# A graph attention layer's first two stages rearranged: layer norm after the projection, node starts counted on TensorE, the score table read in quarters

## What is computed

```
def _L0_gnn_ref(x, edge_index, W, att_src, att_dst, bias, gamma, beta):   # x is already layer-normed
    xh = (x @ W).reshape(N, H, D)                       # H = 8 heads, D = 32
    a_src = jnp.einsum('nhd,hd->nh', xh, att_src)
    a_dst = jnp.einsum('nhd,hd->nh', xh, att_dst)
    ... src, dst = the edges, and a loop on each node
    e = jax.nn.leaky_relu(a_src[src] + a_dst[dst], 0.2)
    m = jax.ops.segment_max(e, dst, N);  e = jnp.exp(e - m[dst])
    alpha = e / segment_sum(e, dst, N)[dst]
    out = segment_sum(xh[src] * alpha, dst, N) + bias
    ... batch norm over the nodes, + x
```

## Time and profile before

| | |
|---|---|
| median of 3 runs | 1977.33 us (1975.37 to 1977.82) |
| profiled execution | 1977.53 us, of which the span from first to last instruction is 1975.8 us |
| first stage | VectorE's next block begins at 100.73 us |
| second stage | the block after it begins at 163.43 us |
| busy over the span | TensorE 69%, GpSimd 56%, VectorE 46%, ScalarE 29% |
| granted TensorE clock, mean | 0.823 of 2.4 GHz |

### The profile page before, as it was taken

How to read it: one execution, slowest core, us unless ns; L and a number is a source line. 1 busy time by engine, 2 the same in 40 slices (tenths; PEclk the granted TensorE clock), 3 DMA queues, 4 the chain that set the end, 5 groups by cost and what they waited for, 6 DMA issues and landing times. The chain is left out here.

```text
span 1975.8 us, 23808 instructions
## 1 busy us (share of the span) xinstructions
PE 1365.6 (69%) x6688; PEld 1134.1 (57%) x6688; DVE 907.3 (46%) x1818; ACT 576.3 (29%) x1264; POOL 1098.3 (56%) x1086
## 2 busy tenths in 40 slices
PE   2435666656666266599999997656666666567998
PEld 2324544444454146599999997444445444346787
DVE  7425544444443667633333333644334333335953
ACT  2133433323333014133333332422222222222310
POOL 4477777777774600377222273077777777773520
PEclk7756878878878575699999999877878787978999
DMA  6484998888887601432111122743333333330002
GB/s 145 119 251 150 298 312 284 281 285 272 276 283 258 155 6 63 134 115 83 46 46 46 46 98 65 174 142 104 105 105 105 105 104 105 106 99 1 1 1 65
DMA packets 156809, 268.56 MB, mean 136 GB/s; under 512 B 26747, under 2 KB 119839, under 8 KB 155567
## 3 DMA queue, kind: packets, MB, share of 16 engines
q1 hardware_dynamic: 100252, 135.75, 22.1%
q0 software_dynamic: 46224, 123.97, 21.0%
q10 hardware_dynamic: 10213, 7.36, 1.5%
HBM read 169.82 MB, written 98.15 MB: 136 GB/s over the span
## 5 line engine op out<-in xcount | busy, mean ns | idle before, releaser
L1182 POOL DMA_INDIRECT sum_rows<-xn_tab,src_e x391 | 373.3, 955 | 174.5 <-issue 118.8
L1207 PE MATMUL bank<-sum_held,sum_hot 128*125 128x256 f32 x976 | 304.1, 474 | 195.3 <-ACT sum_held L1217 191.1
L798 POOL DMA_INDIRECT gat_rows<-xh_tab,src_e x363 | 343.4, 946 | 114.8 <-issue 107.8
L1207 PEld LDWEIGHTS bank<-sum_held,sum_hot 128*125 128x125 f32 x976 | 222.2, 236 | 273.5 <-issue 179.7
L871 PE MATMUL bank<-gat_rows,gat_same 128*128 128x264 f32 x784 | 263.7, 483 | 126.2 <-issue 126.2
L871 PEld LDWEIGHTS bank<-gat_rows,gat_same 128*128 128x128 f32 x784 | 176.6, 244 | 166.4 <-issue 132.6
L1217 ACT COPY sum_held<-sum_rows 128x1024 f32 x122 | 127.4, 1045 | 373.6 <-SPq L1173 334.1
L1894 PE MATMUL bank<-weights,e_xthigh 128*128 x896 | 220.3, 330 | 8.5 <-DVE e_xtlow L2049 5.4
L915 ACT COPY gat_outs<-bank 128x528 f32<-128x528 f32 x196 | 117.3, 598 | 281.8 <-PE bank L871 280.5
L2054 DVE TENSOR_TENSOR e_h<-e_gated,bank 128x342 f32<-128x342 f32 x112 | 57.1, 510 | 262.9 <-ACT e_gated L1987 262.9
L1239 DVE SCALAR_TENSOR_TENSOR res<-bank,prep_inv,res 125x256 f32 x122 | 58.9, 483 | 234.8 <-PE bank L1207 228.2
(11 more groups left out here) (508 smaller groups left out, 2416.8 us busy)
## 6 DMA issues: line engine op xcount, KB each, us to landing
parts<-gat_outs SPq DMA_DIRECT2D x27, 1904.0 KB, 8.0
staged<-w_tab SPq DMA_DIRECT2D x8, 2132.0 KB, 8.9
w_tab<-w_stage SPq DMA_DIRECT2D x16, 682.0 KB, 10.6
w_raw<-in_L_ffn_w_dram SPq DMA_DIRECT2D x16, 640.0 KB
gat_rows<-xh_tab,src_e POOLq DMA_INDIRECT x391, 4.7
sum_rows<-xn_tab,src_e POOLq DMA_INDIRECT x391, 2.8
w_tab<-w_stage SPq DMA_DIRECT2D x8, 768.0 KB, 10.6
weights<-y_tab SPq DMA_DIRECT2D x10, 600.0 KB
```

The source lines that it names most:

```text
L798: pool.indirect_dma_start(out=rows[b % R][:, t, :], out_offset=None, in_=k.xh_tab, in_offset=bass.IndirectOffsetOnAxis(ap=k.src_e[:, b * S ...
L1182: pool.indirect_dma_start(out=rows[:, at // IP % (RING * GPAIRS), at % IP, :], out_offset=None, in_=k.xn_tab, in_offset=bass.IndirectOffse ...
L1207: m = nc.tensor.matmul(k.ps[s][0:P, 0:C], hot[g % 2][:, s, c, :], held[:, s, c, :], start=(c == 0), stop=(c == IP - 1))
```

## The change

First stage:

- `x` is loaded in five chunks, straight behind the edges on SyncE's queue. `dst_pad`, `start_tab`, the 25 window gathers on GpSimd and the 25 passes over all tiles are gone.
- TensorE transposes the raw `x`, tile by tile, and multiplies with a `w` whose column means have been taken off (one matmul with `ones`, two VectorE instructions). VectorE multiplies by `rstd` and adds the bias in one instruction as it takes the result out of PSUM. Layer norm statistics are taken chunk by chunk.
- `starts` are counted otherwise. ScalarE makes `passed` [98, 4, 3125]: the sign of (node - first `dst` of the tile), four `Sign` instructions of 3125 elements, at the head of its list and ahead of all its copies. VectorE makes `rises` [98, 4, 129]: the differences to the tile before, and a column of ones. For each of 25 node tiles TensorE adds four matmuls `passed` x `rises` in PSUM, which gives each node its window of 128 edges and the tile's number. These 100 matmuls come behind the whole projection in TensorE's list. VectorE and ScalarE count in the windows (two of each four tiles each). `end` comes from two small matmuls.
- SyncE stores `xh_tab` chunk by chunk and then `adst_tab`. GpSimd gathers `firsts` (4) behind the 14 gathers of batch 0, still in this block.

Second stage: SyncE loads `sparse` in four quarters, each with its own semaphore; VectorE scans each as it comes (4 x 8 scans of 128), and the transposes and copies go by eighths. The store of `tails` moves from ScalarE's queue to SyncE's, behind the quarters. `joins` is made in `Walk.on_vector` (three VectorE instructions for rows 0 to 7).

```diff
@@ first_phase, tables @@
-        trash = sb("trash", [P, NT, ET])
-        windows = sb("window", [128, NT, EP])
+        neg_first, rises = sb("neg_first", [Q, J]), sb("rises", [Q, J, WIN])      # WIN = 129
+        passed = sb("passed", [Q, J, N])
+        trash = sb("trash", [P, 8, EP])
@@ sync @@
-            sp.wait_ge(edges_f, 1)
-            sp.dma_start(k.dst_pad..., dstq[:, :]).then_inc(pad_out, 16)
-            move(sp, k.res[:, :, :], x, x_in)
+            for c in range(CHUNKS):
+                move(sp, k.res[:, c * TB:(c + 1) * TB, :], x_rows[:, c * TB:(c + 1) * TB, :], x_in[c])
+            sp.dma_start(bias[:, 0:C], ...)
...
+            for c in range(CHUNKS):
+                sp.wait_ge(taken, (c + 1) * TB)
+                move(sp, xh_rows[:, tiles, :], k.xh[:, tiles, 0:XW], xh_done)
+            for c in range(CHUNKS):
+                move(sp, adst_rows[:, tiles, :], k.xh[:, tiles, XW:RW], adst_out)
@@ scalar @@
-            for t in range(DVE_COUNTS, NT):
-                nc.scalar.activation(trash[:, t, :], first_b[0:P, :], ACT.Sign, bias=half[:, t:t + 1], scale=-1.0, ...)
-            norm_roots(k, act, deviations, roots)
+            act.wait_ge(eps_made, 1)
+            nc.scalar.activation(root0[:, :], eps[:, :], ACT.Sqrt)
+            act.wait_ge(numbered, 1)
+            act.wait_ge(firsts_made, 1)
+            for j in range(J):
+                nc.scalar.activation(passed[:, j, :], node_row, ACT.Sign, bias=neg_first[:, j:j + 1]).then_inc(passed_made, 1)
+            for c in range(CHUNKS):
+                for t in range(c * TB, (c + 1) * TB):
+                    ... nc.scalar.copy(xt[:, t % XR], k.ps[t % XR][:, 0:2 * P])
+                    if t % TB == 2: ... activation(k.rstd chunk, spread chunk, ACT.Sqrt, ...).then_inc(roots, 1)
+            for t in range(NT):
+                if t % WG >= BY_DVE:                                              # WG = 4, BY_DVE = 2
+                    nc.scalar.activation(trash[:, t % 8, :], k.ps[t % 8][0:P, 0:EP], ACT.Sign, ..., accum_out=before[:, t:t + 1])
@@ gpsimd @@
-            for t in range(NT):
-                pool.indirect_dma_start(out=windows[:, t, :], in_=k.dst_pad...)
+            nc.gpsimd.iota(node_row, pattern=[[1, N]], ...).then_inc(numbered, 1)
...
             gather_batch(k, pool, 0)
+            pool.wait_ge(adst_out, 32 * CHUNKS)
+            for j in range(J):
+                pool.indirect_dma_start(out=k.firsts[:, j, :], in_=k.adst_tab, ...)
@@ tensor @@
-            for i in range(NT // TB):   # transposes of xn, then matmuls, five by five
+            for c in range(2):
+                nc.tensor.matmul(k.ps[XR - 1][:, 0:RW], k.ones[:, :], w[:, c, :], ...)
+            for t in range(NT + 1):     # two transposes of k.res tile t, then two matmuls of tile t - 1
+                ...
+            pe.wait_ge(passed_made, J)
+            pe.wait_ge(rises_made, 1)
+            for t in range(NT):
+                ... wait for tiles_kept of two groups back
+                for j in range(J):
+                    nc.tensor.matmul(k.ps[t % 8][0:P, 0:WIN], passed[:, j, t * P:(t + 1) * P], rises[:, j, :], ...)
+            nc.tensor.matmul(k.ps[0][0:P, 0:NT], k.ident[0:P, 1:P + 1], start[:, 0:NT], start=True, stop=False)
+            nc.tensor.matmul(k.ps[0][0:P, 0:NT], corner[:, :], start[:, 1:NT + 1], start=False, stop=True)
@@ vector @@
-            for t in range(DVE_COUNTS):
-                v.tensor_scalar(trash[:, t, :], first_b[0:P, :], k.node[:, t:t + 1], None, ALU.is_lt, ALU.add, ...)
+            spreads(0); w -= column means; the five table copies
+            for c in range(CHUNKS):
+                if c < CHUNKS - 1: spreads(c + 1)     # bn_stats x5 and four small ones
+                take(c)                               # xh = ps * rstd + bias, x5
+                if c == 2: ... rises
+            for g in range(GROUPS): ... count in two windows, keep four tile numbers from PSUM
@@ spread_phase, sync @@
-            sp.dma_start(sparse[:, :], edge_rows).then_inc(sparse_in, 16)
+            for j in range(J):
+                sp.dma_start(sparse[:, part], edge_rows[:, part]).then_inc(sparse_in[j], 16)
+            sp.wait_ge(tails_made, 2)
+            move(sp, chain_rows[:, :, C:RW], tails[:, :, :], k.chain_cleared)
@@ gpsimd @@
-            for j in range(J):
-                pool.indirect_dma_start(out=firsts[:, j, :], in_=k.adst_tab, ...)
@@ scalar @@
-            act.wait_ge(tails_made, 2)
-            move(act, chain_rows[:, :, C:RW], tails[:, :, :], k.chain_cleared)
@@ vector @@
-            for h in range(H):
-                v.tensor_tensor_scan(filled[:, h::H], k.cont_q[:, :], sparse[:, h::H], ...)
+            for j in range(J):
+                dve.wait_ge(sparse_in[j], 16)
+                ... copy firsts of quarter j
+                for h in range(H):
+                    v.tensor_tensor_scan(filled_j[:, h::H], k.cont_q[:, j * EP:(j + 1) * EP], of_j[:, h::H], ...)
@@ Walk.on_vector @@
+        me(dve, v.memset(k.joins[0:H, 0:1], 0.0))
+        me(dve, v.tensor_copy(k.joins[0:H, 1:ET], self.bank[0:H, 0:ET - 1]))
+        me(dve, v.tensor_tensor(k.joins[0:H, 1:ET], self.bank[0:H, 1:ET], k.joins[0:H, 1:ET], ALU.is_equal))
```

More of the change, by code:

```diff
@@ L302, in _ @@
+            act.wait_ge(halves_made, 1)
+            for t in range(NT):
+                if t % WG >= BY_DVE:
+                    act.wait_ge(windows, t + 1)
+                    nc.scalar.activation(trash[:, t % 8, :], k.ps[t % 8][0:P, 0:EP], ACT.Sign, bias=half[:, t:t + 1], scale=-1.0,
+                                         accum_out=before[:, t:t + 1]).then_inc(signed, 1)
         @block.gpsimd
@@ new lines, in _ @@
+            for c in range(2):
+                last_mm = nc.tensor.matmul(k.ps[XR - 1][:, 0:RW], k.ones[:, :], w[:, c, :], start=(c == 0), stop=(c == 1))
+            last_mm.then_inc(w_summed, 1)
+            for t in range(NT + 1):
+                if t < NT:
+                    if t == XR - 1:
+                        pe.wait_ge(w_ready, 1)
+                    if t % TB == 0:
+                        pe.wait_ge(x_in[t // TB], 32)
+                    if t >= XR:
+                        pe.wait_ge(xt_made, t - XR + 1)
@@ new lines, in take @@
+            def take(c):
+                rstd = k.rstd[:, c * TB:(c + 1) * TB]
+                dve.wait_ge(roots, c + 1)
+                me(dve, v.reciprocal(rstd, rstd))
+                for t in range(c * TB, (c + 1) * TB):
+                    dve.wait_ge(projected, t + 1)
+                    v.scalar_tensor_tensor(out=k.xh[:, t, :], in0=k.ps[XR + t % XP][0:P, 0:RW], scalar=k.rstd[:, t:t + 1], in1=bias[:, :], op0=ALU.mult, op1=ALU.add).then_inc(taken, 1)
+            spreads(0)
+            dve.wait_ge(w_summed, 1)
```

363 lines of the change are left out of this document (171 added, 192 removed).

## The result

The changed kernel takes 1949.15 us in the median of four runs (1947.08 to 1950.14), beside 1976.35 us of the kernel before (four runs, 1971.5 to 1977.82): a ratio of 0.9859, 95% interval 0.9843 to 0.9876. I had forecast 1959.5 us with a range from 1951.5 to 1968.5.

The account below looks back on a forecast made before the run. GpSimd was taken to set the edge stage's pace, so the ends of the two stages ahead of it counted. The span of 1975.8 us less 12.8 and 5.1, plus 1.7, gave 1959.6, stated as 1959.5 us; range 1951.5 to 1968.5.

Parts of the forecast that it names:

- the price of a window matmul: First stage, TensorE: 200 instructions at 0.16 us each, 32 us, bounds 26 and 34.
- TensorE's chain: First stage: projection to 52.2 us, window matmuls to 84.2, then small work; it ends the stage at 87.9 us.
- The drain: Ends of both stages: a block ends 4.8 us after GpSimd's last indirect DMA starts.
- The slow gathers: Second stage: four gathers under VectorE's scans took 1.93 instead of 0.95 us; the 3.9 us lost was left unchanged.
- Both gains: First stage 12.8 us gained, bounds 7.8 and 17.6; second stage 5.1 us, bounds 0 and 8.
- the first case of the two that I had left open: First stage, ScalarE's head: ready at 18.6 us, or 21.2 if `Sqrt` ahead of `Sign` needs another table load.
- the scores' chain: Second stage: quarter loads, scans, transposes and copies, done 54.8 us into the block, ahead of GpSimd's 57.6.
- Rival A: Second stage: the store of the tails on SyncE ends at 62.4 us, nothing gained there: 1964.7 us; chance 0.1.
- B: First stage: the 200 matmuls run at the lower clock level, 52 us: 1979.6 us, no change; chance 0.04.
- C: First stage: TensorE stays at the lower clock level through projection and windows: 2008 us, slower; chance 0.03.
- D: First stage: VectorE's or ScalarE's head much later than 24 us, 5 us more: 1965 us; chance 0.08.
- TensorE's projection: First stage: 25 tiles at 1.21 us, 30.2 us, plus 1 us for beginning at the lower clock level.

Follow-up runs that it names:

- e1: The kernel before with only the new first stage, its second stage and `firsts` as they were: 1955.05 us, ratio 0.9887.
- e4: The changed kernel, `sparse` still loaded in quarters but scanned by 8 scans of 512 once all have landed: 1957.48 us, ratio 0.9906.
- e14: The changed kernel once more, unaltered: 1948.27 us, ratio 0.9857 to the kernel before.
- e5c: The changed kernel with the four `firsts` gathers put back behind the 25 scatters of the second stage: 1952.90 us, ratio 0.9881.
- e11: The changed kernel with last store split, 70 idle TensorE matmuls, and VectorE taking three tiles before its second statistics: 1949.40 us, ratio 0.9862.
- e20: The changed kernel with bias loaded behind the first chunk of `x`, split last store and 70 idle matmuls: 1951.45 us, ratio 0.9867.
- e18: The changed kernel with early bias load, split store and 70 idle matmuls: 2301.35 us, ratio 0.9831, where the kernel before took 2339 us.
- e17: The changed kernel with early bias load, split store and 70 idle matmuls: 2303.46 us, ratio 0.9818, where the kernel before took 2339 us.

## Why the prediction was wrong

**The step that failed** is the price of a window matmul, "I take 0.16: 32 us, bounds 26 and 34". It is 0.112 us and 22.3 us, under the lower bound; twice the matmuls, at 0.110 each, confirm it. The number came from the earlier trace rows, read wrongly. The busy time of a short run holds the tail of its last instruction, which the next one would cover: L369 has a mean of 273 ns and a pace of 112. The right price stood in the trace of before. L2258, which I took at 0.17, ran as four runs of four, the first of them

```profile
1905.27 0.61 PE L2258 MATMUL bank<-t_ut,att_w_fx 128*128 128x128 f32 x4
```

and (0.61 - 0.275) / 3 = 0.112 us. For L994, one run of eight, it is (2.1 - 0.44) / 7 = 0.24 us at the lower level, half of it 0.12, where I had 0.13. And L359's ten instructions in 1.60 us have a stop of 0.39 us in their middle; the first six start 0.105 to 0.111 us apart. With the right price TensorE's chain would have come out at 52.2 + 22.3 + 3.3 = 77.8 us (measured: 76.51), and the sum would have gone by GpSimd: 85.1, not 87.9. That is 2.8 us of the 4.8 that I missed here, and also the statement on which engine ends the stage. It is not all of the miss: two more terms were mis-sized.

**The drain**, "a block whose last engine is GpSimd ends 4.8 us after its last indirect DMA starts", is 3.39 us in a block of 18 instead of 39: 1.4 us. I had two nearly equal rows, from blocks with 39 and 43 indirect DMAs, and took them for a constant. The remaining 0.6 us is the start of the last indirect DMA, 79.67 and not 80.3: last `xh` done at 51.64, 1.1 us earlier than forecast, 0.2 us more from there to the first gather, 0.2 more in the 18.

**The slow gathers**, 3.9 us "left as it is", shrank to 0.7 (three at 1.17 or 1.16 us). They were 3.7 us in truth, one of the four having taken 1.76 and not 1.93, so 3.1 us less, all that I missed of the second stage (57.6 against 54.5) and the largest single term. The rule that I had cited from the Trainium skill (SBUF — State Buffer, "The single rule") said this; I wrote "toward 1 us" beside the sum and left it out of it. The Trainium skill puts it there with a condition that I left out, that the GpSimd instruction reads SBUF. The three lengths of scan agree with the rule: the delay never exceeds one scan. The same section of the Trainium skill says that DMA never contends with a compute engine unless GpSimd makes its descriptors; the slowed instructions here are those.

**The range.** Both gains came out at what I had named as their best, 17.67 against 17.6 and 8.20 against 8, which gives 1952, just inside the range. What lies below it is 1.5 us in everything behind the two stages, less than the scatter of that part, and 1.0 us between the profiled run and the median; of both I had counted 0.2.

**What was right.** GpSimd's pace, and that it sets the edge stage (452.8 us from its first gather to its last, 452.7 before). The start of the projection, 21 forecast, 19.9 measured, with ScalarE's head done at 18.0 (forecast 18.6) and no second table load, the first case of the two that I had left open. Quartering frees the scores' chain (forecast 54.8 us into the block, measured 136.68 - 83.06 = 53.6), and without it that chain sets the end: e1 and e4 both show it. Rival A was near: SyncE's wait for the tails ended 3.7 us before the block did. B and C did not come: the granted clock reads 1.00 through projection and windows, and but for the first two tiles the pace agrees. D did not come either.

**What I got right by luck.** I gave TensorE's projection 31.2 us and it took 31.0 (19.9 to 50.9), but by other terms: 25 tiles at 1.13 us and not 1.21 are 28.3 us and not 30.2, the first two at half the pace added 2.3 and not 1, and a wait for VectorE, which I had not seen, 0.7. I had put all of it on TensorE. TensorE does set the pace from the sixth tile on, but the bias set when that began: it arrives behind all of `x`, VectorE takes no row without it, and five banks are all that TensorE can fill before that. Where the clock was up early this cost 3.3 us (e14) and ate what the clock had brought.

## What to carry to other kernels

Price a pipelined instruction by the pace within a long group (from start to start), never by the busy time of a short one; where only short runs are at hand, take one instruction's own time off the time of one unbroken run and divide by one less. A group's line can be the sum of several runs, so look at the timeline first. When a stage's end is worth a few microseconds, ask of every small load which bulk load it is queued behind: a load of 1 KB per partition held two engines here. And a piece of work moved from one stage to another pays only if the engine that ends the one isn't the engine that ends the other.

## What the runs showed of the hardware

- The end of the first block, counted from the start of GpSimd's last indirect DMA, costs more the more of them it has issued there: 3.4 us with 18, 4.0 with 32 (14 of which had been issued 42 us before), 4.9 with 43, 5.1 with 46. In the second block, with 39 or 43, it was 4.8 to 5.6 us, and the number doesn't explain the difference.
- `Sqrt` and then `Sign` on ScalarE took one table load of 1.28 us, ahead of both, in the changed kernel, and the `Sqrt` behind the `Sign` at 22.76 us none. In the kernel before, with `Sign` first, there were two loads, at 7.87 and 22.66 us.
- An indirect DMA that falls under VectorE's scans is held up by less than one scan, and not always: by at most 0.98, 0.49 and 0.22 us under scans of 1.13, 0.60 and 0.33 us.
- The record of the granted clock says 1.00 for 19.9 to 24.2 us in the changed kernel, while four instructions took 2.15 and 2.02 us and 1.08 later; where TensorE worked from 2.9 us on, the record for the same pace says 0.50. Early in a trace the pace of the instructions tells the clock, not the record.
- TensorE's clock rose at different times in runs of the same kernel: first tile in 2.15 us in the first and third profile of the changed kernel, in 1.15 us in the second. Of the eleven profiles at ordinary speed with this head and no idle matmuls, two went into the matmuls with `ones` (L335) without a wait, and both had the first tile in 1.15 us (e1, e14); of the nine that waited there 0.37 to 1.40 us, one had (e5c), the others took 2.15.
- With 70 idle matmuls it was 1.15 us in both profiles at ordinary speed (e11, e20), in e18 1.15 and then 1.98, and in e17, which waited 2.76 and 2.03 us on the way, 2.15. In e20 TensorE had waited 2.44 us just ahead of that tile. So whether filling the wait is what kept the clock up is not shown.
